# Order of the first loads, a wait ahead of the gathers of x, and the slots of short blocks, in a graph attention kernel

## The reference

```
q, k, v = x @ Wq + bq, x @ Wk + bk, x @ Wv + bv          # 8 heads of 16
scores  = sum(q[dst] * k[src], -1) / 4 + (edge @ We + be)
probs   = softmax of scores over the edges of one target, by head
agg     = segment_sum(probs * v[src], dst)
out     = layernorm(x + agg @ Wo + bo)
```

## Time and profile before

| what | us |
|---|---|
| median of 3 runs | 2609.24 (2606.43 to 2611.74) |
| the profiled execution's own time | 2600.53 |
| its span, first to last instruction | 2598.6 |

### The profile page before, as it was taken

The page is one execution under the profiler, slowest core; times in us unless marked ns, Lnnn a source line. Parts: engine busy times, 40 slices in busy tenths (PEclk is TensorE's granted clock), DMA queues, the critical chain, the costliest instruction groups (busy, mean ns, idle before and its releaser), DMA issues.

```text
span 2598.6 us, 31022 instructions
## 1 busy us (share of the span) xinstructions
PE 1413.5 (54%) x9783; PEld 946.5 (36%) x9783; DVE 1352.6 (52%) x3156; ACT 430.0 (17%) x1439; POOL 1498.5 (58%) x1572
## 2 busy tenths in 40 slices
PE   5265455555554554546555545555554555555557
PEld 4133243333333343333333333334333333333334
DVE  4254454545554554555555545545454555455556
ACT  1011111111111111111111111111111111111112
POOL 4725565555656566655656555656665665656540
PEclk7556675666666666666666766656676667566767
DMA  6423333333333334333433333343333333333320
GB/s 250 149 75 101 118 104 115 105 102 121 108 117 104 117 103 122 106 119 101 124 99 118 106 100 119 105 122 102 121 104 119 101 121 104 119 105 112 113 84 7
DMA packets 115162, 288.47 MB, mean 111 GB/s; under 512 B 45909, under 2 KB 53856, under 8 KB 107960
## 3 DMA queue, kind: packets, MB, share of 16 engines
q0 software_dynamic: 74624, 203.26, 26.5%
q1 hardware_dynamic: 37628, 76.52, 9.0%
q10 hardware_dynamic: 2748, 6.69, 0.7%
HBM read 274.69 MB, written 11.67 MB: 110 GB/s over the span
## 4 chain that ended last, share of the span: by engine, by line
another core or an unknown queue 36%; PE 32%; DVE 20%; issue 9%; ACT 2%; DVEq 0%; ACTq 0%; DMA 0%
PE q_banks L1215 11%; PE ps_a L1252 7%; DVE prod L833 4%; DVE score L844 4%; PE ps_e L1227 2%; PE ps_t L1192 2%; PE ps_s L1273 2%; DVE wv L854 2%; DVE run_fwd L896 1%; PE ps_a L1294 1%; PE ps_t L1198 1%; PE ps_s L1279 1%; PE ps_a L1304 1%; DVE cand L890 1%
## 5 line engine op out<-in xcount | busy, mean ns | idle before, releaser
L508 POOL DMA_INDIRECT kv_buf<-kv_table,src_i x1536 | 1469.0, 956 | 1020.5 <-DVE wv L854 582.8
L1215 PE MATMUL q_banks<-q_blk,hots 64*128 64x128 f32 x3128 | 417.6, 406 | 462.9 <-issue 225.2
L598 ACT ACTIVATE hots<-ps_t 128x512 f32<-128x512 f32 x377 | 225.1, 597 | 1974.8 <-PE ps_t L1198 962.6
L1215 PEld LDWEIGHTS q_banks<-q_blk,hots 64*128 64x128 f32 x3128 | 319.9, 278 | 582.3 <-issue 562.4
L833 DVE TENSOR_TENSOR prod<-q_banks,kv_buf 128x512 f32<-128x512 f32 (+1 forms) x392 | 269.0, 686 | 379.2 <-remote 251.4
L854 DVE TENSOR_TENSOR wv<-kv_buf,ps_w 128x512 f32<-128x512 f32 (+1 forms) x392 | 265.8, 679 | 356.5 <-remote 333.9
L1252 PE MATMUL ps_a<-wv,hots 128*64 128x136 f32 x3128 | 375.4, 378 | 5.4 <-ACT wv L639 4.8
L1294 PE MATMUL ps_a<-sums_sb,carry_from 128*1 128x136 f32 x112 | 34.1, 406 | 530.3 <-DVE sums_sb L964 524.1
L844 DVE TENSOR_REDUCE score<-prod 128x32 f32<-128x512 f32 (+1 forms) x392 | 267.3, 682 | 7.7
L1252 PEld LDWEIGHTS ps_a<-wv,hots 128*64 128x64 f32 x3128 | 239.2, 183 | 68.2 <-issue 52.1
L1294 PEld LDWEIGHTS ps_a<-sums_sb,carry_from 128*1 128x1 f32 x112 | 4.8, 81 | 551.9 <-DVE sums_sb L964 545.4
(11 more groups left out here) (155 smaller groups left out, 1403.4 us busy)
## 6 DMA issues: line engine op xcount, KB each, us to landing
edge_f<-in_edge_blk SPq DMA_DIRECT2D x55, 1024.0 KB
kv_buf<-kv_table,src_i POOLq DMA_INDIRECT x1536
kv_table<-kv_buf ACTq DMA_DIRECT2D x12, 512.0 KB, 2.8
xt_blk<-in_x_t SPq DMA_DIRECT2D x114, 32.0 KB
out<-y_out SPq DMA_DIRECT2D x114, 32.0 KB
kv_buf<-in_x_perm SPq DMA_DIRECT2D x5, 512.0 KB
codes<-code_table SPq DMA_DIRECT2D x108, 10.5 KB
code_table<-kv_buf SPq DMA_DIRECT2D x1, 1344.0 KB
```

Source lines behind the costliest of these rows:

```text
L508: pool.indirect_dma_start(kv_buf[:, b % NBUF, t, :], None, kv_table, bass.IndirectOffsetOnAxis(ap=src_i[:, column:column + 1], axis=0)).th ...
L598: one = act.activation(hots[:, v % 2, :, :].rearrange("p k n -> p (k n)"), ps_t[:, :], ACT.Relu, bias=1.0)
L1215: one = pe.matmul(ps_q[j][:, k * D:(k + 1) * D], hots[own, (v - 1) % 2, 0, k * P:(k + 1) * P], q_blk[own, b % QBUF, :], start=True, stop=True)
```

## The change

On SP, the load of `row_i` moves from behind the third chunk of x to behind the seventh. On GpSimd, the gathers of x wait for the fifth chunk of x to have landed as well as for the indices. On ScalarE, everything that reads `row_i` moves from ahead of the first three stores of the table to ahead of the fifth, sixth and seventh (`CODED_FROM` is 4; there are 13 groups). In the main loop, a block gets as many slots as it or the block ahead of it has steps, and at least four: with these sizes all blocks keep 7 but the last, which gets 4, and there are 413 slots instead of 427. A block is finished after its own number of steps instead of after seven. What is made ahead of a chain is made at the same offsets as before, or later where the block has fewer slots.

```diff
+    SPACE = [SLOT if b == 0 else max(GS[b], GS[b - 1], 4) for b in range(NB)]
+    BASE = [sum(SPACE[:b]) for b in range(NB + 1)]
...
+        SLOT_OF = {BASE[b] + g: q for q, (b, g) in enumerate(STEPS)}
+        BACK_SLOT_OF = {BASE[b + 1] + LAG + g: q for q, (b, g) in enumerate(STEPS)}
...
         def chain(v, offset):
-            b, g = divmod(v - SLOT - offset, SLOT)
-            return b if 0 <= b < NB and g == 0 else None
+            return BASE.index(v - offset) - 1 if v - offset in BASE[1:] else None
+
+        def ahead(v, offset, latest):
+            for b in range(NB):
+                if v == BASE[b + 1] - min(offset, SPACE[b] - latest):
+                    return b
 
         def at_node(v, offset):
-            return chain(v, LAG + SLOT + offset)
+            for b in range(NB):
+                if v == BASE[b + 1] + LAG + GS[b] + offset:
+                    return b
...
             for k, (lo, hi) in enumerate(XCHUNKS):
                 sync.dma_start(xt[:, lo:hi], x_perm[:, lo:hi]).then_inc(s_xt[k], 16)
-                if k == min(2, len(XCHUNKS) - 1):
-                    sync.dma_start(row_i, dst_row).then_inc(s_row, 16)
+            sync.dma_start(row_i, dst_row).then_inc(s_row, 16)
             sync.dma_start(src_i[:, T:NT], src_blk[:, T:NT]).then_inc(s_src, 16)
...
             pool.wait_ge(s_srcfirst, 16)
+            pool.wait_ge(s_xt[min(4, len(XCHUNKS) - 1)], 16)
             for g, (t0, t1) in enumerate(STEP[0]):
...
-            act.wait_ge(s_row, 16)
-            for k in range(2):
-                one = act.activation(row_less[:, k:k + 1], row_i[:, ROW:ROW + 1], ACT.Identity, bias=less_c[0:ROWS, k:k + 1], scale=-1.0)
-            one.then_inc(s_rowcode, 1)
-            act.wait_ge(s_rowcode, ROWCODE["less"])
+            CODED_FROM = min(4, len(GROUPS) - KNOWN)
 
             def code_edges(k):
                 if k == 0:
+                    act.wait_ge(s_row, 16)
+                    for i in range(2):
+                        one = act.activation(row_less[:, i:i + 1], row_i[:, ROW:ROW + 1], ACT.Identity,
+                                             bias=less_c[0:ROWS, i:i + 1], scale=-1.0)
+                    one.then_inc(s_rowcode, 1)
+                    act.wait_ge(s_rowcode, ROWCODE["less"])
...
             for j, (n, count, parts, shared) in enumerate(GROUPS):
-                code_edges(j)
+                if j >= CODED_FROM:
+                    code_edges(j - CODED_FROM)
                 act.wait_ge(s_staged, HALVES_TO[j + 1])
...
-                    if chain(v, -4) is not None:
-                        copy_terms(chain(v, -4))
+                    if ahead(v, 4, 2) is not None:
+                        copy_terms(ahead(v, 4, 2))
...
-                    if chain(v, -2) is not None:
-                        runs_of_dst(chain(v, -2))
+                    if ahead(v, 2, 4) is not None:
+                        runs_of_dst(ahead(v, 2, 4))
...
-                    if chain(v, -5) is not None:
+                    if ahead(v, 5, 1) is not None:
                         for g in range(EGROUPS):
-                            edge_terms(chain(v, -5), g)
-                    if chain(v, -2) is not None:
-                        turn_terms(chain(v, -2))
+                            edge_terms(ahead(v, 5, 1), g)
+                    if ahead(v, 2, 3) is not None:
+                        turn_terms(ahead(v, 2, 3))
```

More of the change, by code:

```diff
@@ L344, in columns, with step_back @@
             return slice(FIRST_TILE[b] + t0, FIRST_TILE[b] + t1)
+        SLOT_OF = {BASE[b] + g: q for q, (b, g) in enumerate(STEPS)}
+        BACK_SLOT_OF = {BASE[b + 1] + LAG + g: q for q, (b, g) in enumerate(STEPS)}
         def step_in(v):
-            b, g = divmod(v, SLOT)
-            return FIRST[b] + g if 0 <= b < NB and g < GS[b] else None
+            return SLOT_OF[v] if v in SLOT_OF else None
+        def step_back(v):
+            return BACK_SLOT_OF[v] if v in BACK_SLOT_OF else None
         def chain(v, offset):
-            b, g = divmod(v - SLOT - offset, SLOT)
-            return b if 0 <= b < NB and g == 0 else None
+            return BASE.index(v - offset) - 1 if v - offset in BASE[1:] else None
[3 more added lines that the diff above has]
+                    return b
         def at_node(v, offset):
-            return chain(v, LAG + SLOT + offset)
+            for b in range(NB):
+                if v == BASE[b + 1] + LAG + GS[b] + offset:
+                    return b
         def steps_over(b, upto):
             return FIRST[b] + sum(1 for t0, _ in STEP[b] if t0 < upto)
-        SLOTS = range(SLOT * (NB + 2) + LAG + 9)
+        SLOTS = range(BASE[NB] + LAG + GS[NB - 1] + 9)
         def hots_in(v):
-            return step_in(v + 1), step_in(v - SLOT - LAG)
+            return step_in(v + 1), step_back(v)
         HOT_SLOTS = [v for v in range(-1, SLOTS[-1]) if hots_in(v) != (None, None)]
@@ L373, in steps_to, with steps_back_to @@
         def steps_to(v):
-            return sum(1 for b in range(NB) for g in range(GS[b]) if b * SLOT + g <= v)
+            return sum(1 for u in SLOT_OF if u <= v)
+        def steps_back_to(v):
+            return sum(1 for u in BACK_SLOT_OF if u <= v)
         def after(engine, name, semaphore, value):
@@ L410, in load_codes @@
                 if b >= CBUF:
-                    last = (b - CBUF) * SLOT + GS[b - CBUF] - 1
-                    sync.wait_ge(s_matched, HOTS_TO[last + SLOT + LAG])
+                    sync.wait_ge(s_matched, HOTS_TO[BASE[b - CBUF + 1] + LAG + GS[b - CBUF] - 1])
                 n = HALF[b] * P
@@ L676, in _ @@
                         copy_projected(at_node(v, 5))
-                    if step_in(v - SLOT - LAG) is not None:
-                        copy_weights(step_in(v - SLOT - LAG))
-                    if chain(v, -4) is not None:
-                        copy_terms(chain(v, -4))
+                    if step_back(v) is not None:
+                        copy_weights(step_back(v))
+                    if ahead(v, 4, 2) is not None:
+                        copy_terms(ahead(v, 4, 2))
                     if at_node(v, 7) is not None:
@@ L995, in _ @@
                 for v in SLOTS:
-                    if chain(v, -2) is not None:
-                        runs_of_dst(chain(v, -2))
-                    if step_in(v - SLOT - LAG) is not None:
-                        weigh(step_in(v - SLOT - LAG))
+                    if ahead(v, 2, 4) is not None:
+                        runs_of_dst(ahead(v, 2, 4))
+                    if step_back(v) is not None:
+                        weigh(step_back(v))
                     if step_in(v) is not None:
@@ L1239, in sum_step @@
             def sum_step(v):
-                q = step_in(v - 1 - SLOT - LAG)
+                q = step_back(v - 1)
                 b, g = STEPS[q]
```

6 lines of the change are left out of this document (3 added, 3 removed).

## The result

The changed kernel takes 2617.15 us (median of 20 runs, 2608.01 to 2631.27) and the kernel before, run beside it, 2606.97 us (20 runs, 2600.34 to 2613.60). The ratio is 1.0044, 95% interval 1.0029 to 1.0060: **slower by 0.44%, 10 us between the medians (11.5 by the ratio)**, where 2 us less had been forecast, and above the range. The profiled execution took 2615.65 us with a span of 2613.6, against 2600.53 and 2598.6 before. One fact is needed to read all that follows: the comparisons ran on several chips, and their times lie on two levels. On some the kernel before takes 2607 to 2616 us, on the others 2024 to 2028 us. The text calls them two kinds of chip; whether the difference lies in the chip or in something else that went on there isn't shown. Each table row names its own kernel before, and times are not compared across.

What follows compares the result with a forecast made beforehand. No engine was taken as the bound, but waits, with the main loop's start hanging on the gathers' end. +0.3 + 0 + 0 - 2, about -2 us, made the profiled 2600.53 into 2598.5, as a median 2607; range 2595 to 2615.

Steps and rivals of the forecast that it cites:

- The middle untouched: Between prologue and end: slots, offsets and engine order as before, cost nothing; a difference over 5 us would refute it.
- Part one: Prologue: gathers of x wait for five chunks, starting 8 us later; last table addition at 58.0 instead of 57.65, +0.3 us.
- the trade: Prologue: each microsecond of gather delay buys one of undisturbed additions, near zero net; 2602 to 2612 us, chance 0.35.
- the release: Prologue: held-up table additions come loose 4.6 us after the last gather of x, at 52.4 instead of 44.33 us.
- the gap: Prologue: first pause over 2 us between VectorE's table additions, forecast after 12 to 15 of them instead of five.
- my reading: Prologue: while GpSimd issues gathers back to back, TensorE's signals reach others late, one in 3.5 to 10 us.
- late signals: Prologue: TensorE's signals arriving late at other engines under GpSimd's gathers; VectorE waited some 26 us for seemingly finished work.
- Part two: Prologue: row codes later, the 0.9 MB load behind x and ScalarE's passes moved into idle time; 0, bounds 0 and +3.
- Part three: End: fewer slots put block 56's run maxima ahead of block 55's weighing; about -2 us, bounds -6 and +1.
- Faster: Rival, prologue: additions get through before the gathers of x end, block 1 starts earlier; 2595 to 2603, taken 2599, chance 0.40.
- Slower: Rival, prologue: full DMA starts the stall, so it begins as before but ends later; 2617, or 2615, chance 0.13.
- Bystanders: Rival, prologue: gathers hold up nobody, GpSimd's delay hides in 21.7 us idle, end gives -2; 2607, chance 0.12.

Runs made afterwards that it cites:

- slots_six: The kernel before with the change's slots only, but at least six slots per block instead of four: 2618.46 us against 2615.86, ratio 1.0009.
- codes_only: The kernel before with only the row load and code passes moved later, no wait for the fifth chunk: 2023.78 us against 2023.71, ratio 1.0001.
- prologue_only: The kernel before with both prologue edits (row codes later, gathers of x behind the fifth chunk), old slots: 2028.62 us against 2023.71, ratio 1.0022.
- slots_only: The kernel before with only the change's slots and finishes, old prologue: 2028.59 us against 2023.71, ratio 1.0022.
- changed_again: The whole changed kernel once more, beside the kernel before: 2619.14 us against 2615.86, ratio 1.0004.
- hold_again: The kernel before with GpSimd's gathers of block 2 held until the main loop's first product: 2603.53 us against 2615.86, ratio 0.9950.
- wait_only: The kernel before with only GpSimd's wait for the fifth chunk, row load and code passes early: 2030.01 us against 2023.71, ratio 1.0028.
- chain_moved: The kernel before with the change's fewer slots, but each block finished after seven as before: 2028.96 us against 2024.17, ratio 1.0020.
- finish_moved: The kernel before with seven slots for all blocks, each finished after its own steps: 2025.56 us against 2024.17, ratio 1.0003.

## Why the prediction was wrong

**The middle untouched: right as far as can be told.** My own test (over 5 us refutes it) tripped, at 5.6. But slots_six, whose first 55 blocks run as before, has 2410.3, the changed kernel itself has 2411.9 and 2416.8, and the other kind of chip gives 1927.7 to 1928.8 for the gathers of codes_only, prologue_only and slots_only. The test was set tighter than two executions of this kernel repeat.

**Part one (+0.3): the trade is there where signals are late, its size is unsettled.** The fifth chunk was there at 10.97 (about 11 was forecast), the release came 4.6 us behind the last gather, and the last addition at 59.2 and, in changed_again, 58.15 (58.0). The additions ahead of the gap were fewer than forecast: 12 by idle time, but ten by the measure that gave five before, where 12 to 15 had been named. Missed: the first gather takes 1.11 us instead of 3.09 when it waits, so all ended at 45.84, not 47.8, and ten additions were left open instead of seven. That "their 21.7 us of idle time cover the 8 us" fits the starts of block 1 where there are 21.7 us (64.03 and 62.00 against 61.5 to 64.2); where the cover is 2.87 us the same edit costs 4.0 to 4.9. I had named the cover and not its price if it is gone.

**The rule that spoke against my reading** (the Trainium skill, SBUF — State Buffer, "Who interferes with whom": a DMA never contends with a compute engine) fits one kind of chip: in codes_only additions begin every 0.86 us under the gathers. On the other, hold_again's 0.03 us against 7.2, from one profile each, ties the late signals to the gathers. What does it, a memory, a queue or the path of the signals, no run here tells.

**Part two (0): right**, 1.0001. It is also what lets the wait end at 11 instead of 14 us: wait_only costs 6.3 us and prologue_only, in the same comparison, 4.9.

**Part three (-2): this is the step that failed.** I wrote that the run maxima of 56 going ahead of the weighing of 55 was "only exchanged for other work" and that VectorE "is done with the carry of block 56 at about 2581", so that the end came out shorter. For the exponentials of 56 the exchange held, and there may even be a gain: 33.1 against 34.5 us behind those of 54 at the same clock, in one profile against four. What failed is that the price of what the chain passed was put at nothing. VectorE runs its instructions in order, and behind the chain stand the weighings of 55; both scans now lie between the first two of them (2577.48 and 2581.95). From the last weighing of 54 to the last of 55 it is 11.0 to 11.4 us in the seven profiles with the new slots, against 6.9 to 8.3 in the twelve with the old. Those weighings feed the sums and the finishes that end the kernel. The reciprocal of 54's finish comes 30.7 to 31.4 us behind the exponentials of 54 instead of 24.0 to 26.3, and its projection so stands on TensorE ahead of the sums of 56, for which the last weighing waits 3.12 us. In the changed kernel's profile the carry was ready 9.5 us behind the exponentials of 56 instead of 5.0. The one gain that I had counted there is real, the carry's product starts 0.14 us behind the carry instead of 3.3, but on a carry that is late. In all it is 5 us more behind the exponentials of 56, and +4.8 to +5.4 us measured, where I had bounds of -6 and +1.

The wait of 1.04 us for TensorE is not what makes the price. In its old place the same scan waits longer, 1.33 to 1.34 us in the eleven other profiles; this is codes_only:

```profile
1994.99 1.28 DVE L917 TENSOR_TENSOR_SCAN ps_s<-seq_far,seq_left,ps_s 8x512 f32<-8x512 f32 x1 [1.34 <-PE ps_s L1276]
```

That the chain's slots are the cause is shown by chain_moved and finish_moved. How the 5 us divide among the instructions that were passed is read from the order of the rows; no run varied it.

**The rivals.** Faster: the additions did not get through; in the stretch additions still began 5 to 10 us apart. Slower: it named 2615 to 2617, but from a stretch that begins at the same time, which it did not. The number was nearly right for a wrong reason. Bystanders: on one kind of chip the gathers are that, but there is no 21.7 us of idle time there to hide the delay in. No rival had the end of the kernel as its place.

## What to carry to other kernels

Moving a chain ahead on an in-order engine is an exchange only for that engine's own time. Ask whether what it passes leads to the end of the kernel, and follow that to the next engine's queue, down to the last store. A start that is delayed is free only while the engine behind it has idle time; read that idle time on the machine that counts, since here it was 21.7 us on one chip and 2.9 on another. And before a few microseconds of a profile are given a cause, look at how far two executions of the same code differ in that stretch, and at the granted clock of both.

## What was not expected of the hardware

The same kernel takes 2607 to 2616 us on some chips and 2024 to 2028 on others, with nearly the same busy times: GpSimd 1498.5 us in the earlier trace rows and 1491.1 in codes_only, VectorE 1352.6 and 1342.7. What causes it no run shows; the profiles differ in waiting. Ahead of 169 of its 1536 gathers from the table GpSimd waits for VectorE's weighing, 582.8 us in all, on the one kind (kernel before), and ahead of 6 of them, 1.8 us in all, on the other (codes_only), from the waits of GpSimd:

```profile
POOL kv_buf L508 <- DVE wv L854: 582.8, 169, 39.0
```

```profile
POOL kv_buf L507 <- DVE wv L857: 1.8, 6, 0.3
```

A first indirect gather takes 3.09 us when it starts at 3 us and 1.11 when it starts at 11 (before and after); why is not shown.
